# Attention scores on TensorE: key pieces of 32 columns in place of chunks of 125

## What is computed

```python
q = proj(hs, Wq, bq, S); k = proj(at, Wk, bk, T); v = proj(at, Wv, bv, T)
scores = jnp.einsum('bhsd,bhtd->bhst', q, k) / sqrt(32)
scores = jnp.clip(jnp.where(attend, jnp.clip(scores, -50, 50), -10000), -50, 50)
probs = softmax(scores)
ctx = jnp.einsum('bhst,bhtd->bhsd', probs, v)
delta = rs * (ctx @ Wo.T + bo)     # then a layer norm
```

## Time and profile before

| | before |
|---|---|
| median of 3 runs (lowest to highest) | 1606.23 us (1600.45 to 1606.64) |
| the profiled execution's own time | 1606.45 us |
| its span in the profile | 1604.4 us |
| TensorE matmuls busy | 1491.7 us, 93% |
| VectorE, ScalarE, GpSimd busy | 1036.6, 643.3, 531.3 us |
| granted TensorE clock, mean | 0.969 |

### The profile page before, as it was taken

One profiled execution on the slowest core, in us unless ns is written; L12 is line 12 of the kernel. 1 busy time (PEld: TensorE's weight loads), 2 busy tenths in 40 slices (PEclk: granted clock), 3 DMA queues, 4 the chain that ended last, 5 costly groups with the idle time before them and its releaser, 6 DMA issues. The chain is left out here.

```text
span 1604.4 us, 33621 instructions
## 1 busy us (share of the span) xinstructions
PE 1491.7 (93%) x13352; PEld 1150.3 (72%) x13352; DVE 1036.6 (65%) x2051; ACT 643.3 (40%) x834; POOL 531.3 (33%) x488
## 2 busy tenths in 40 slices
PE   7999999996999999999999999999999963998994
PEld 3688888875887877788787887878788742554652
DVE  2766666644266767677666766767676673775797
ACT  2233333331333333333333333334333321989761
POOL 0000000000144444443444444444443443651552
PEclk9999999998899999999999999999999976999997
DMA  6022222223212121211212111121211103276953
GB/s 203 27 82 86 95 95 95 96 99 114 75 43 64 36 73 36 69 40 39 70 36 73 36 54 55 36 73 36 73 36 43 48 14 86 70 275 258 360 159 93
DMA packets 61748, 138.53 MB, mean 86 GB/s; under 512 B 4674, under 2 KB 29762, under 8 KB 59906
## 3 DMA queue, kind: packets, MB, share of 16 engines
q1 hardware_dynamic: 61698, 137.84, 26.4%
HBM read 93.78 MB, written 44.04 MB: 86 GB/s over the span
## 5 line engine op out<-in xcount | busy, mean ns | idle before, releaser
L700 POOL TENSOR_TENSOR xa_psum<-xa_pr 125x448 f32<-125x448 f32 x128 | 147.2, 1150 | 464.9 <-DVE xa_pr L840 464.9
L873 PE MATMUL xa_bKV<-xa_cx,wA 128*128 128x376 f32 x1536 | 289.5, 338 | 7.4 <-DVE xa_cx L766 7.4
L886 PE MATMUL xa_bKV<-wZ,xa_cx 128*125 128x512 f32 x1152 | 289.2, 399 | 0.0
L873 PEld LDWEIGHTS xa_bKV<-xa_cx,wA 128*128 128x128 f32 x1536 | 266.7, 189 | 21.9 <-issue 13.1
L886 PEld LDWEIGHTS xa_bKV<-wZ,xa_cx 128*125 128x125 f32 x1152 | 208.7, 186 | 55.1 <-issue 10.6
L786 DVE RECIPROCAL xa_rinv<-xa_bPV 128x112 f32<-128x112 f32 x128 | 109.5, 855 | 160.8 <-PE xa_bPV L927 160.8
L750 ACT ACTIVATE xa_pr<-xa_bSC 125x1344 f32<-125x1344 f32 x128 | 165.5, 1293 | 74.4 <-PE xa_bSC L941 74.4
L729 ACT ACTIVATE xa_kf<-xa_bKV,xa_bk 128x376 f32<-128x376 f32 x128 | 73.6, 575 | 297.7 <-PE xa_bKV L873 297.6
L840 DVE TENSOR_SCALAR xa_pr<-xa_pr,xa_keep 125x448 f32<-125x448 f32 x384 | 151.5, 451 | 43.7 <-ACT xa_pr L750 43.7
L703 POOL TENSOR_TENSOR xa_psum<-xa_psum,xa_pr 125x448 f32<-125x448 f32 x128 | 157.1, 1227 | 12.3 <-POOL xa_psum L700 4.4
L735 ACT COPY xa_v<-xa_bKV 125x512 f32<-125x512 f32 x96 | 56.4, 588 | 203.8 <-PE xa_bKV L886 203.8
(11 more groups left out here) (167 smaller groups left out, 2164.1 us busy)
## 6 DMA issues: line engine op xcount, KB each, us to landing
wraw<-in_ctxT SPq DMA_DIRECT2D x32, 752.0 KB, 5.6
ff_hr<-h_scratch SPq DMA_DIRECT2D x4, 3584.0 KB, 15.2
wraw<-in_w SPq DMA_DIRECT2D x8, 1024.0 KB, 7.6
sa_raw<-in_x SPq DMA_DIRECT2D x8, 896.0 KB, 5.9
x_scratch<-sa_qraw SPq DMA_DIRECT2D x8, 896.0 KB, 5.1
xa_qf<-q_scratch SPq DMA_DIRECT2D x32, 224.0 KB, 5.5
xa_x<-x_scratch SPq DMA_DIRECT2D x32, 224.0 KB, 5.0
x_scratch<-xa_x SPq DMA_DIRECT2D x32, 224.0 KB, 2.3
```

Of the source, the lines that this page charges most:

```text
L700: nc.gpsimd.tensor_tensor(psum01[:], third(h, 0), third(h, 1), ALU.add).then_inc(p01_ok, 1)
L873: mm = nc.tensor.matmul(bKV[par][:, 0:TP], w["k"][l][:, c, m * P:(m + 1) * P], cx[par][r][:, c, :], start=c == 0 and k == 0, stop=c == C - ...
L886: mm = nc.tensor.matmul(bKV[1 - par][0:TW, 0:D], cx[par][l][:, c, t * TW:(t + 1) * TW], w["v"][r][:, c, :], start=c == 0 and k == 0, stop= ...
```

## The change

The inner matmul over a chunk's 125 stationary columns becomes four, of 32, 32, 32 and 29 columns. Each reads its own piece of the key chunk and writes its own 32 (or 29) PSUM partitions of the same bank and columns; the moving operand is the same for the four. Rows still come from `j`, so rows and columns of the array are both cut into four. Ahead of the scores of each head TensorE increments a new semaphore, `sc_go`, on which nobody waits.

```diff
--- before.py
+++ after.py
@@ -621,7 +621,7 @@
         x1_in, q_in, x2_out = ([n.sem(f"{k}{p}") for p in range(2)] for k in ("x1_in", "q_in", "x2_out"))
         const_ok, rs_ok, top_ok = n.sem("const_ok"), n.sem("rs_ok"), n.sem("top_ok")
         chi_ok, clo_ok = n.sem("chi_ok"), n.sem("clo_ok")
-        k_done, v_done, k_ok, v_ok = n.sem("k_done"), n.sem("v_done"), n.sem("k_ok"), n.sem("v_ok")
+        k_done, v_done, k_ok, v_ok, sc_go = n.sem("k_done"), n.sem("v_done"), n.sem("k_ok"), n.sem("v_ok"), n.sem("sc_go")
         sc_done, exp_ok, pr_ok, p01_ok, ps_ok = n.sem("sc_done"), n.sem("exp_ok"), n.sem("pr_ok"), n.sem("p01_ok"), n.sem("ps_ok")
         pv_done, sum_done, ri_ok, at_ok, cthi_ok, ctlo_ok = n.sem("pv_done"), n.sem("sum_done"), n.sem("ri_ok"), n.sem("at_ok"), n.sem("cthi_ok"), n.sem("ctlo_ok")
         o_done, dl_ok, st_ok, mv_ok, ve_ok, rstd_ok, rr_ok = n.sem("o_done"), n.sem("dl_ok"), n.sem("st_ok"), n.sem("mv_ok"), n.sem("ve_ok"), n.sem("rstd_ok"), n.sem("rr_ok")
@@ -935,11 +935,14 @@
                         pe.wait_ge(q_in[par], 8 * (b - par) + 16)
                     pe.wait_ge(k_ok, s + 1)
                     wait(pe, exp_ok, s)
+                    pe.sem_inc(sc_go)
                     for t in range(TC):
                         for j in range(NJ):
                             own = slice(j * HD, (j + 1) * HD)
-                            mm = nc.tensor.matmul(bSC[0:TW, j, t * S:(t + 1) * S], kf[own, h, t * TW:(t + 1) * TW], qf[par][own, h, :],
-                                                  start=True, stop=True)
+                            for lo in range(0, TW, HD):
+                                hi = min(lo + HD, TW)
+                                mm = nc.tensor.matmul(bSC[lo:hi, j, t * S:(t + 1) * S], kf[own, h, t * TW + lo:t * TW + hi],
+                                                      qf[par][own, h, :], start=True, stop=True)
                     mm.then_inc(sc_done, 1)
 
                     if h > 0:
```

## The result

The changed kernel takes 1716.6 us in the median of four runs, against 1605.7 us for the kernel before: ratio 1.0671, 95% interval 1.0643 to 1.0699. One of the four was a slow run of 2967 us; the ratio leaves it out, and the median of the other three (1706.15 to 1718.3 us) is 1714.9 us, which is what this text compares with: slower by 109 us. The forecast was 1620 us with a range up to 1685. It had the direction and missed the size: 14 us were expected where 109 came.

The account below looks back on a forecast made before the run. TensorE was taken to bound the kernel, its time in the cross-attention loop being kernel time nearly one for one. 1606.45 + 10 (instruction starts) + 4 (loop body fetched again) = 1620 us, range 1598 to 1685.

Parts of the forecast that it names:

- The array: Score matmuls in cross-attention: 6 rounds a head before and after, moving operand 112 columns either way; nothing to gain.
- Loads: Score weight loads: 183 ns at 125 columns, 109 ns at 32; the part of the change that can win.
- The waits and the increment: Waits for k_ok and exp_ok move to the sc_go increment ahead of the scores: cost nothing, at most 6 us.
- Starts: Scores of each head: a load with its matmul starts every 6.7 ns, 0.73 us first to last start, +10 us.
- The bound above, 8 ns a pair: Upper bound for starting a score load with its matmul: +0.20 us a head x 128 = +26 us.
- The loop body: TensorE's cross-attention loop grows to 2435 instructions; 13 jumps may wait for a packet, 0 to 18 us, taken +4 us.
- the clock stays at 1.00: Changed cross-attention loop: TensorE's busy time rises 0.6 us an iteration and its granted clock stays at full level.
- Starts are cheap: Rival, 25%: loads set the scores' pace; a head takes 0.57 to 0.62 us, -4 to -10 us, 1597 to 1602.
- Four side by side: Rival, 17%: score pieces of the same rows hold each other up; 1.24 us a head, 1682, or 2.3 us, 1818.
- The instructions don't come in time: Rival, 13%: loop jump waits at the upper end, 1635; with a stop inside a head too, up to 1650.

## Why the prediction was wrong

*Right.* TensorE is the bound of this loop, and its time is the kernel's. The array gained nothing. Loads fell from 183 to 103 ns (109 forecast). The waits and the increment are free. L918, away from the jumps, and exp take as long as before. The body outgrew what stays, the records are 12288, and eleven packets an iteration come where about ten were named.

*The step "Starts", +10 us, was mis-sized.* I took a pair of instructions to start every 6.7 ns to the end. That holds for the first 14 tiles or so. Then the pace is set by places that come free when old matmuls end, and a tile needs 17 ns between the pauses and 26 with them: 1.15 us from first to last start, not 0.73. In time that is +0.48 us a head, 61 us over 128; 44.6 were measured, since L899's wait (0.48 us a batch) went and hid 15. The sum had no term for that gain either. The bound above, 8 ns a pair, was worked out from a head of 48 instructions, which lies under the limit and could not show it. Nothing in the rows had more in flight. I should have widened the upper bound for that reason: a pace read from a short burst is no bound for a burst four times as long.

*The step "The loop body", +4 us, was right in kind and sixteen times too small; it is the larger of the two misses.* I costed one packet at 1.1 to 3.4 us, less the 2.0 us that the engine had in hand, and took 0.3 us bare. The branch takes 3.36 to 3.90 us, at the upper end or over it, and leaves 1.65 to 2.19 us bare, above my highest 1.4. A second packet isn't there in time either (up to 1.03 us), and then the clock falls, 2.6 us more in the mean of the thirteen jumps. The rows of the queue could not tell the second and third of these; "the clock stays at 1.00" is the sentence that failed. The Trainium skill, "Runtime: NRT & Kernel Launch", Instruction fetch mechanics, gives 2048 instructions for TensorE and a stall at a jump to what has gone. The runs agree in kind, that such a jump stalls, and not in the number: 1721 stay, and 1913, which 2048 would hold, don't. That whole packets count and the body rarely begins at one would explain the difference; no run shows it. I had put the +4 into the sum and too low a price on it.

*The rivals.* "Starts are cheap" (25%) fell with 1.15 us; the 4 ns a tile of the Trainium skill, "TensorE: Matmul & The Clock Gate", Part 3, stands against 6.7 ns here for the first 14, and 17 to 26 ns after them. "Four side by side" (17%) gave nearly the right head, 1.24 us, by luck: sixteen tiles do start within 0.12 us, and changing the order left the head as it was. "The instructions don't come in time" (13%) named the sign that the trace shows, idle of over 0.5 us behind each jump, and stopped at 1650. Two separate losses came together: some 45 us of heads, 46 by the heads' own rows (61 - 15), and some 66 us of jumps, 65 by the trace's idle stretches and clock. No case of mine paired a head of over 1 us with a dear jump.

## What to carry to other kernels

Cutting the stationary columns of matmuls that already fill the array four abreast adds no throughput and multiplies instructions by four; count the instructions of a group as well as its array time, and look at the pace beyond the first 32 pairs. Count the loop body too: here one of 1721 instructions stayed, those of 1913 and more cost 5 to 7 us at every jump, and writing the loop out took that back. A stall on a bound TensorE can cost about twice its length, if the clock falls behind it: here 31 us of idle engine came with 33 us of clock.

## What was not expected of the hardware

TensorE held 32 loads with 32 matmuls in flight and no more: 32 matmul records (16 fp32 matmuls of two passes) started within 235 ns, and the loads behind them came 31 to 32 ns after the first tile's passes had ended, in the order of the program (with 56 columns, where a matmul ends earlier, the 34th load came 46 ns sooner). A jump back to instructions that have gone took 3.3 to 3.6 us in the median in five kernels, with small tiles and without. And the granted clock behind the same kind of stall fell in some iterations of a kernel and not in others.
